# Adding the mask of cross-attention's scores in TensorE, in the last group of a decoder layer

## The reference

```
x = layernorm(x + self_attention(x))           # 32 heads of 16
x = layernorm(x + cross_attention(x, ctx, mask))
x = layernorm(x + ffn(x))                      # sign weights, routed input and output scales

def cross_attention(q, ctx, mask):             # 32 query heads, 8 key/value heads, keys = values = ctx
    scores = einsum('bsgrd,btgd->bgrst', xq, xk) / sqrt(16) + mask      # mask: 128 x 128, the same for all
    probs = softmax(scores)
    return einsum('bgrst,btgd->bsgrd', probs, xv)
```

## Time and profile before

| what | value |
|---|---|
| median of 3 runs | 406.38 us (402.18 to 407.63) |
| the profiled execution, own time | 409.41 us |
| its span in the trace | 407.6 us |
| busy in the span: PE, DVE, ACT, POOL | 84%, 66%, 38%, 28% |
| mean granted clock of PE, share of full | 0.864 |

### The profile page before, as it was taken

How to read it: one execution, slowest core, us unless ns; L and a number is a source line. 1 busy time by engine, 2 the same in 40 slices (tenths; PEclk the granted TensorE clock), 3 DMA queues, 4 the chain that set the end, 5 groups by cost and what they waited for, 6 DMA issues and landing times.

```text
span 407.6 us, 7606 instructions
## 1 busy us (share of the span) xinstructions
PE 341.6 (84%) x2661; PEld 244.0 (60%) x2661; DVE 267.6 (66%) x974; ACT 153.7 (38%) x293; POOL 113.0 (28%) x203
## 2 busy tenths in 40 slices
PE   1693789997889999997999999879899965699563
PEld 1692556795647758975567499666556743444342
DVE  0968653558757648688785497878756777804444
ACT  3852135420144854302375733023755520046220
POOL 3362400131240314433422155421121431000321
PEclk9998568998895999996999999959999976579755
DMA  8948800167570001784510026955000155000001
GB/s 282 374 152 241 183 4 6 56 191 220 145 185 5 12 22 57 206 248 122 167 55 5 0 82 192 260 134 160 5 14 2 44 145 142 4 2 2 0 1 51
DMA packets 26703, 42.59 MB, mean 104 GB/s; under 512 B 8153, under 2 KB 18529, under 8 KB 24361
## 3 DMA queue, kind: packets, MB, share of 16 engines
q1 hardware_dynamic: 26393, 41.58, 36.1%
q10 hardware_dynamic: 272, 0.52, 0.3%
HBM read 29.32 MB, written 12.32 MB: 102 GB/s over the span
## 4 chain that ended last, share of the span: by engine, by line
PE 65%; DVE 20%; issue 5%; DMA 4%; ACT 3%; POOL 2%; SPq 0%; POOLq 0%; DVEq 0%; ACTq 0%
DVE x L778 8%; PE bank_a L883 7%; PE bank_a L884 7%; PE bank_a L885 7%; PE bank_a L962 4%; PE bank_a L932 4%; PE bank_b L1027 4%; PE bank_b L1016 4%; PE bank_a L949 3%; PE bank_b L1017 3%; PE bank_b L1019 3%; PE bank_b L1062 3%; PE bank_b L1063 3%; DVE nma L714 2%; PE bank_b L1004 2%
## 5 line engine op out<-in xcount | busy, mean ns | idle before, releaser
L778 DVE CUSTOM_DVE_ANT_0 x<-bank_b,mraw 128x128 f32<-128x128 f32 x256 | 59.0, 287 | 9.3 <-PE bank_b L1004 2.6
L596 ACT ACTIVATE pb<-bank_b 128x512 f32<-128x512 f32 x64 | 37.6, 600 | 61.7 <-PE bank_b L1019 44.0
L588 ACT ACTIVATE pa<-bank_a 128x512 f32<-128x512 f32 x64 | 37.5, 597 | 26.2 <-PE bank_a L949 13.8
L714 DVE TENSOR_REDUCE nma<-bank_a 128x4 f32<-128x512 f32 x64 | 39.9, 681 | 6.7 <-PE bank_a L932 6.5
L883 PE MATMUL bank_a<-xH,wH 128*128 128x256 f32 x128 | 37.6, 294 | 3.4 <-DVE xL L686 3.4
L1016 PE MATMUL bank_b<-idr,mH 128*128 128x512 f32 x64 | 36.9, 576 | 0.6 <-DVE nmb L778 0.5
L884 PE MATMUL bank_a<-xL,wH 128*128 128x256 f32 x128 | 37.0, 289 | 0.0
L885 PE MATMUL bank_a<-xH,wL 128*128 128x256 f32 x128 | 36.9, 288 | 0.0
L1004 PE MATMUL bank_b<-kx,qx 96*128 96x128 bf16 x256 | 27.0, 252 | 11.5 <-DVE nmb L778 8.9
L932 PE MATMUL bank_a<-ks,qs 96*128 96x128 bf16 x256 | 25.2, 250 | 11.0 <-DMA ks<-scr_k 8.9
L1004 PEld LDWEIGHTS bank_b<-kx,qx 96*128 96x128 bf16 x256 | 18.5, 112 | 20.9 <-DVE nmb L778 12.9
(11 more groups left out here) (160 smaller groups left out, 738.5 us busy)
## 6 DMA issues: line engine op xcount, KB each, us to landing
wraw<-in_L_attn_attn_qkvw_dram SPq DMA_DIRECT2D x3, 1024.0 KB, 8.7
scr_q<-qp SPq DMA_DIRECT2D x8, 384.0 KB, 3.1
qs<-scr_q SPq DMA_DIRECT2D x8, 384.0 KB, 4.5
scr_k<-kp SPq DMA_DIRECT2D x8, 384.0 KB, 4.2
ks<-scr_k SPq DMA_DIRECT2D x8, 384.0 KB, 4.9
scr_x<-xp SPq DMA_DIRECT2D x8, 384.0 KB, 2.7
qx<-scr_x SPq DMA_DIRECT2D x8, 384.0 KB, 4.0
qs<-scr_q SPq DMA_DIRECT2D x8, 256.0 KB, 4.6
```

What stands on the lines that cost most here:

```text
L714: dve.tensor_reduce(nma[:, b, 4 * j:4 * j + 4], pa_bank(i, *step)[:].rearrange("p (m t) -> p m t", m=KT), AX.X, ALU.max, negate=True).then ...
L778: last = dve.tensor_tensor_reduce(x2[:, b, r * P:(r + 1) * P], pb_bank(i, *step)[:, r * P:(r + 1) * P], mraw[:], -1.0, -LOWEST, ALU.add, A ...
```

## The change

For the steps s of the last group (i = 3 = MASKED), PE starts each bank with two matmuls of 512 columns, weights `idr` (identity), moving operand `mH` and then `mL`, repeated for the four heads; the four score matmuls are added to it. DVE takes the four maxima with one `tensor_reduce` of 128x512 from PSUM. It no longer waits for its own step before, nor for the output store, and writes no scratch. Groups 0 to 2 are as they were.

```diff
+MASKED = NG - 1
@@ vector: thread B, step s @@
                     b, g = step[1:]
                     rb.wait_full(dve, i, *step)
+                    if i >= MASKED:
+                        dve.tensor_reduce(nmb[:, b, :].rearrange("p (h k) -> p h k", k=KT)[:, 4 * (g % 2):4 * (g % 2) + 4, g // 2],
+                                          pb_bank(i, *step)[:].rearrange("p (r t) -> p r t", r=4), AX.X, ALU.max,
+                                          negate=True).then_inc(*rb.is_empty(i, *step))
+                        continue
 
                     if g > 0:
                         rb.wait_emptied(dve, i, "s", b, g - 1)
@@ tensor: thread B, step s @@
                         pe.wait_ge(x_stacked[b], 48 * (i + 1))
                         pe.wait_ge(c_stacked[b], 48 * (i + 1))
+                    if i >= MASKED:
+
+                        d4 = dst[:].rearrange("p (r t) -> p r t", r=4)
+                        for part in (mH, mL):
+                            pe.matmul(d4, idr[:], part[:].rearrange("p (o t) -> p o t", o=1).broadcast_to([P, 4, P]),
+                                      start=part is mH, stop=False)
                     for r in range(4):
                         last = pe.matmul(dst[:, r * P:(r + 1) * P], qx[0:SR, b, 4 * (g % 2) + r, g // 2, :], kx[0:SR, b, g, :],
-                                         start=True, stop=True)
+                                         start=i < MASKED, stop=i < MASKED or r == 3)
                     last.then_inc(*rb.is_full(i, *step))
```

## The result

The changed kernel takes 402.11 us (median of 22 runs), the kernel before 405.65 us in the 22 runs beside it: ratio 0.9924, 95% interval 0.9898 to 0.9950, or 3.1 us less. The forecast was -2.0 us; rival 1, the held clock, was -3.8 us. The interval, 2.0 to 4.1 us less, holds both, so only the traces can part them.

The account below looks back on a forecast made before the run. VectorE was taken to pace the last group's score steps, TensorE from 354 us on. Terms: -0.8 us (second sequence), -3.0 (transposed steps), +1.8 (clock) = -2.0, so 406.38 becomes 404.4 us; range 400.4 to 408.4.

Parts of the forecast that it names:

- rival 1: Last group's score steps: TensorE keeps full clock through the wait for ldx:1; -3.8 us (-0.8 and -3.0); chance 0.25.
- the 1.8 us charged for the clock: Second sequence onward: about four microseconds of dense TensorE work at half clock, costing 1.8 us.
- First sequence lost in ldx:1: Last group's first sequence: some 2.5 us of VectorE gain ends waiting for ldx:1; s:1,0 starts 1.2 us later.
- a new step at half clock: Last group's score steps with mask matmuls: 1.28 us each when TensorE runs at half clock.
- Two new steps at 0.69 us: Last group's score steps at full clock: 0.23 + 0.23 + 0.225 = 0.69 us each, paced by TensorE.
- more than 0.23 us at full clock: Sign of being wrong in kind: mask matmuls in the score steps costing more than 0.23 us at full clock.
- I take it that it falls there: TensorE's clock falls at about half load, 344 to 348 us, around the 2 us wait for ldx:1.
- Transposed steps: 3.0 us foreseen: st:0,0 to st:0,4 at full instead of half clock: 4.9 steps, 0.61 us less each, 3.0 us.
- cover of 0.8 us: Ahead of st:1,0: third row of maxima lands at 360.0, wanted at 360.8, so its transfer costs nothing.
- the estimate from them was 0.59 us a step: New score step from the skill's matmul spacings: 2 x 0.131 + 4 x 0.081 us, with VectorE still setting the pace.
- HAM oscillation — how this bites in real kernels: Skill's rule applied to the wait before s:1,0: waiting for a transfer lowers TensorE's clock, so the next block starts slow.

## Why the prediction was right, and where it was off

- **Direction and range: right.** -3.1 us against the forecast -2.0, in the range and within 2%. That it lies near is in part luck: the 1.8 us charged for the clock were not paid, while the new steps cost more and the transposed steps gave less than reckoned.
- **First sequence lost in ldx:1: right, shown.** L833 ended 1.5 and 1.2 us later than before (predicted 1.18), s:1,0 started 1.3 and 1.1 us later (predicted 1.2), and freeing the load gave it back. Two sizes in it were off and nearly cancelled: a new step at half clock takes 1.42 us and not 1.28, so ff:1 started 1.5 us later; and s:1,0 followed the end of L833 after 5.9 and 5.8 us, not 6.05. The prediction also gives the third transfer of before 4.8 us, which was the second's; the third took 4.7.
- **Two new steps at 0.69 us: too low.** They came every 0.76 us, so the second sequence took 6.3 us and not 5.9. The pair of mask matmuls is 0.52 in the chain, not 0.46: in the timeline the first starts 0.31 us before the second, the second 0.24 before the scores. By the prediction's own sign ("more than 0.23 us at full clock") this part was wrong in kind, though it is worth only 0.4 us in the second sequence.
- **Clock: the step that failed** is "I take it that it falls there". It held through the wait for ldx:1 in both profiles, so rival 1 was the right mechanism and the forecast's 1.8 us for a lost clock were not paid. Why it held stays open. PE was busy 2.35 us of four around that wait (339.35:343.35, above); with mask matmuls from s:0,2 on it was busy 2.31 us, in all groups 2.27 us, and in both the clock fell. These lie too close together to tell the cases apart. I had no row between 1.4 and 3.9 us and should have given both outcomes like chances.
- **Transposed steps: 3.0 us foreseen, 2.1 to 2.3 found.** Of the missing 0.7 us 0.3 are in the first five steps and what stands between them: 7.7 us before, 5.0 after, in the first profiles. The other 0.4 are the stacking of the maxima, whose cover of 0.8 us was not there. The third row landed 3.3 us after its issue at 353.6, not 1.9 as in the earlier trace rows, so at 356.9, and st:1,0 started at 357.1, 0.4 us late:
```profile
L421 SPq DMA_DIRECT2D qx<-mrb x3: 503/591/592, 352.4 to 353.6; - x3
...
DMA to landing us min/median/max: 1.8/1.9/3.3
```
  It was 3.4 us in the second profile. What came between is another transfer: one packet of 16 KB of instructions. The table of queues for 354:356 has it, at 3.7% of sixteen engines' 2 us, that is 1.2 us of one engine, beside the third row:
```profile
q8 instruction: 1, 0.02, 3.7%
...
qx<-mrb SPq DMA_DIRECT2D x1, 8.0 KB, 3.3
```
  The packet runs from 354.55 to 355.74, and the last three packets of the third row start at 355.73 to 355.79; all the others had started by 355.1. In the second profile and in the kernel with the load freed (3.0 us) the same packet stands in the same place; in the ten other profiles none lies within this row's transfer, and it landed after 1.9 us. No run moved the packet by itself.
- **Rival 1's sum.** -3.8 was to be -0.8 and -3.0; it came as -0.4 and -2.3 (second profiles: -0.7 and -2.1), with 0.2 to 0.3 us more gained behind st:1,0.
- **The Trainium skill's figures** (TensorE: Matmul & The Clock Gate, Back-to-back issue gap): the estimate from them was 0.59 us a step. The trace disagrees: 0.76 us, further from it than my 0.69. Its account of a clock lost in a wait for a transfer (HAM oscillation — how this bites in real kernels), weighed for the forecast, tells it of waits of about 3 to 5 us. The prediction carried it over to one of 2 us, which the section doesn't state. In both profiles of the changed kernel, with waits of 1.65 and 1.55 us, it did not come; in the kernel with the change in all groups the clock fell after one of 1.73 us.

## What to carry to other kernels

Where two engines share a loop and TensorE idles in it, price a shift of work at both clock levels: work added to TensorE may cost nothing where the clock is kept for what follows, and work taken off may gain nothing. Which level comes is not sure even for the same instructions, so carry both sums. Then follow each shortened stretch to its next condition; here a load whose wait was a shared buffer took all that the first sequence gained. And before comparing two spans, line the traces up at the first changed instruction: here 4.8 of the 7.8 us between them lay ahead of it.

## What was not expected of the hardware

- The stage from group 1's first projection to group 2's has the same instructions in both kernels. In the kernel before the clock was at half from 122.3 to 132.5 (second profile 121.9 to 132.1), in the changed one not at all there, in its second profile from 120.2 to 123.6; that stage took 81.8, 81.8, 78.9 and 80.1 us. Differences of this size can be part of the spread of several microseconds between runs of one kernel; no run here parts them from other causes.
- A load of instructions can hold up a small transfer of data: the third 8 KB row of the maxima landed 1.9 us after issue in ten profiles and 3.0 to 3.4 us in the three where a 16 KB packet of instructions, 1.0 to 1.3 us long, lay in its way. A change that moves a transfer in time can move it into such a load.
- The final feed-forward products, back to back, didn't bring the clock back in the kernel before (0.50 in 390:400); in the changed kernel it came back from 393.8 to 397.2, and in the one with the load freed from 388.5 to 395.4. What decides it these runs don't show.
